# A graph network on one core: a sum moved one round later in VectorE's order, six result slots in the convolutions, a counting table of 128 by 784

## The chip, the core and the metric

The kernel runs on one core of a Trainium2 chip. A core has TensorE (matmuls and transposes into PSUM banks), VectorE, ScalarE, GpSimd (here it issues the indirect DMAs, gathers and scatters) and SyncE (it issues all other DMAs). Each engine works through its own instructions in order and waits on semaphores; 16 DMA engines move the data. The metric is the time of one launch in microseconds, the median of several runs.

## The reference

`x` has 100000 rows of 96 numbers; there are 50000 edges, sorted by destination. Four layers, each with a residual sum:

```python
edge_index = jnp.stack([src, dst])
h = jnp.maximum(_layernorm(x, axis=-1), 0.0)
x = x + _L0_gnn_ref(h, edge_index, edge_attr_32, ...)   # first edge layer
h = jnp.maximum(_layernorm(x, axis=-1), 0.0)
x = x + _L1_gnn_ref(h, ..., edge_attr_96, src, dst)     # second edge layer
h = jnp.maximum(_layernorm(x, axis=-1), 0.0)
x = x + _L2_gnn_ref(h, edge_index, W, b)                # convolution 0
h = jnp.maximum(_layernorm(x, axis=-1), 0.0)
x = x + _L3_gnn_ref(h, src, dst, ...)                   # convolutions 1, 2, 3
```

The first edge layer, where the moved sum lies (`h = x + update` there is the kernel's `y`):

```python
edge_input = jnp.concatenate([x[src], edge_attr], axis=-1)
messages = _gelu(edge_input @ mW1 + mb1) @ mW2 + mb2
gates = jax.nn.sigmoid(_gelu(edge_input @ gW1 + gb1) @ gW2 + gb2)
aggregated = jax.ops.segment_sum(messages * gates, dst, num_segments=x.shape[0])
combined = jnp.concatenate([x, aggregated], axis=-1)
update = _gelu(combined @ uW1 + ub1) @ uW2 + ub2
h = x + update
# then a layer norm of h with ln_g, ln_b
```

The convolutions gather a source row for each edge, scale it by the root of the source's degree, sum over the edges of a destination, apply a 96 by 96 weight and scale by the root of the destination's degree. Out-degrees and in-degrees are needed for all nodes.

## The kernel before, in words

**Stages, one after another.** Setup; counting (the degrees of all nodes as a table); the table's steps; a dense stage (all 100000 nodes as if they had no edges, in 196 groups); the two edge layers `e0`, `e1` and the four convolutions `conv[0]` to `conv[3]`, each over 98 groups of 512 edges (`G` = 4 columns of 128). Between stages a table in device memory (`t1`, `t2`, `c1`, `c2`) must be complete before the next stage gathers from it.

**The order.** `pipelined(eng, n, stages)` (L109) writes one engine's program as rounds: in round r it calls each stage function in the order of the list for group r - lag. So the lists are the order, and a function that waits holds everything behind it on that engine. `need(eng, count, value)` is a wait on a counter; `g.at(k)` is a slot of k; `landed`, `freed` give values of DMA counters.

**First edge layer, one round.** GpSimd gathers the source and destination rows, eight gathers of 128 rows a group (L598), at most five groups ahead of ScalarE's `norm`. VectorE: `times_g` (`yx`, L1214), `times_gate` (`msgT`, L1301), `new_x` (`xo`, L1336), `sums` (the scan into `aggT`, L1281), `edge_moments` (of the gathered rows), `new_y` (`y`, L1317, from PSUM bank 7), `with_b` (L1327), `moments_y`, then `of_round`: eleven short steps (L1148 to L1170) that give the roots `rstd`, `nmr` for the gathered rows and for `y` at once. ScalarE: `evac_d`, `update_act`, `hidden` (`g` L782, `m` L785), `edge_y` (`yg`, L722, needs the roots), `half_gate` (tanh, L796), `norms` (`hs`, `hd`, L687, need the roots), `evac_s`. TensorE: `hid`, `upd_u` (L993, the source of `new_y`), `messages`, `upd_z`, `tr`. SyncE stores `xo` at lag 10.

**Convolutions, one round.** GpSimd gathers four times (L598); ScalarE scales the rows (`rows_in`, L831 or L834); TensorE transposes them and after the scan (`sums`, L1281) applies the weight (L1017); VectorE's `finish` (L1415, L1422) writes the result into one of three slots of `xo`, for which it waits until the store of the group three before has landed (`x_out`, or in convolution 3 the four scatters, L673). SyncE loads `goes`, `idx` and, from convolution 1 on, `now` (`now_load`, L544: the degree roots of sources, plane 0, and destinations, plane 1, in one DMA for three groups, after `xr` of three groups ago) and stores at lag 9 (`conv_store`, L562). In convolutions 0 and 1 every third round has the eleven root steps (`row_roots`).

**Counting.** 392 rounds. A node number is split into `hi` and `lo` (shift and mask on integers, `LO` = 1024). VectorE compares `iota_lo` with `lo` (two comparisons of 1024 columns, L1081), ScalarE makes the row of `hi` (two squares L695, one relu L699, 128 columns wide), both into two buffers in turn; TensorE adds the products into four banks (four matmuls of 512 columns with 98 weight columns, L861). The table then takes some twenty steps on 98 partitions and 1024 columns (L1090 to L1125).

## Time and profile before

| | us |
|---|---|
| median of 3 runs | 7310.7 (7306.1 to 7322.6) |
| the profiled execution | 7306.9 |
| its span on the core | 7305.1 |
| busy: TensorE, VectorE, ScalarE, GpSimd | 4615.6, 4007.5, 3526.0, 4164.3 |
| first gather of the dense stage, of `e0`, of `e1` | 564.2, 2147.1, 3565.3 |
| first gather of conv 0, 1, 2, 3 | 4575.7, 5127.3, 5718.8, 6281.6 |

No engine is busy for more than 63% of the span, and the granted clock of TensorE is 0.716 on the mean. The stages have different limits, so shares over the whole span say little: each stage is read by itself, and in it what ends the idle time ahead of each engine's instructions.

### The profile page before, as it was taken

What the parts mean: (1) busy time and instruction counts of PE and PEld (TensorE: products, weight loads), DVE (VectorE), ACT (ScalarE), POOL (GpSimd) and SP (SyncE); (2) the same over time, 40 slices, a digit from 0 to 9 for tenths busy, and PEclk for the clock granted to TensorE, in tenths of its full rate; (3) what the DMA queues carried; (4) which work ended last, traced back from release to release, by engine and by line L of the source; (5) the groups of instructions that cost most, each with busy time, mean ns of one, the idle gap of its engine ahead of it and who ended that gap; (6) DMA issues with size and microseconds to landing.
All of it is one profiled execution on the core that took longest, in us unless ns stands there. A gap on an engine that the chain in (4) does not pass through costs nothing. (4 is left out here: it accounts for less than half of the span.)

```text
span 7305.1 us, 104580 instructions
## 1 busy us (share of the span) xinstructions
PE 4615.6 (63%) x19614; PEld 2994.2 (41%) x19614; DVE 4007.5 (55%) x12715; ACT 3526.0 (48%) x8822; POOL 4164.3 (57%) x4323
## 2 busy tenths in 40 slices
PE   6877888888876666666687888455445455322222
PEld 2335565556543333333344444344344344322222
DVE  5776777777765555555455555566555433322222
ACT  6886888888865555555455555222222122111110
POOL 0004555555447555554377776776666566677777
PEclk9997888998878877777688888555555555555555
DMA  0002333333332222222244444566444688533333
GB/s 15 0 0 77 100 102 103 101 105 100 100 89 69 62 60 58 61 61 59 64 118 118 120 120 110 142 159 157 102 115 112 102 122 121 93 72 78 76 80 72
DMA packets 956422, 652.69 MB, mean 89 GB/s; under 512 B 728867, under 2 KB 833199, under 8 KB 956232
## 3 DMA queue, kind: packets, MB, share of 16 engines
q1 hardware_dynamic: 818346, 483.05, 23.6%
q0 software_dynamic: 137984, 168.67, 14.6%
q8 instruction: 27, 0.44, 0.0%
q14 instruction: 65, 0.53, 0.0%
HBM read 420.24 MB, written 232.62 MB: 89 GB/s over the span
## 5 line engine op out<-in xcount | busy, mean ns | idle before, releaser
L1017 PE MATMUL bank<-w,aggT 96*128 96x96 f32 (+1 forms) x3136 | 790.2, 433 | 1343.8 <-DVE aggT L1281 1343.7
L598 POOL DMA_INDIRECT got<-info_d,idx x784 | 776.9, 991 | 1310.3 <-issue 779.5
L598 POOL DMA_INDIRECT xs<-t,idx x1176 | 1110.1, 944 | 626.7 <-issue 346.2
L1017 PEld LDWEIGHTS bank<-w,aggT 96*128 96x128 f32 (+1 forms) x3136 | 698.5, 328 | 1498.3 <-issue 1323.8
L598 POOL DMA_INDIRECT xs<-c,idx x784 | 756.9, 965 | 347.9 <-issue 233.3
L834 ACT ACTIVATE msg<-xs,now 128x96 f32<-128x96 f32 x784 | 227.7, 363 | 1340.0 <-DMA xs<-c,idx 535.3
L1281 DVE TENSOR_TENSOR_SCAN aggT<-goes,aggT,bank 96x512 f32<-96x512 f32 (+1 forms) x490 | 621.1, 1267 | 74.8 <-PE bank L977 45.4
L598 POOL DMA_INDIRECT xs<-in_x_dram,idx x392 | 375.5, 958 | 489.1 <-ACT hd L687 327.9
L687 ACT ACTIVATE hd<-xd,nmr,rstd 128x96 f32<-128x96 f32 x1568 | 599.2, 454 | 32.7 <-DVE nmr L1170 32.7
L1010 PE MATMUL bank<-ident,msg 128*96 128x128 f32 (+1 forms) x1568 | 420.3, 423 | 224.9 <-ACT msg L831 172.6
L935 PE MATMUL bank<-ident,hs 128*128 128x128 f32 (+1 forms) x784 | 173.5, 361 | 586.8 <-ACT hs L687 585.2
L1422 DVE SCALAR_TENSOR_TENSOR xo<-bank,now,rows 128x96 f32<-128x96 f32 x784 | 194.5, 311 | 551.1 <-DMA c<-xo 333.8
L1422 DVE SCALAR_TENSOR_TENSOR y<-bank,now,rows 128x96 f32<-128x96 f32 x392 | 97.3, 310 | 721.3 <-issue 370.9
L861 PE MATMUL bank<-xd,hot_hi 128*98 128x512 f16 x1568 | 407.3, 382 | 83.3 <-ACT hot_hi L699 69.9
L673 POOL DMA_INDIRECT out_dram<-xo,idx_out x392 | 390.2, 995 | 119.3 <-issue 119.3
L598 POOL DMA_INDIRECT xd<-in_x_dram,idx x392 | 381.8, 974 | 119.5 <-issue 119.2
L598 POOL DMA_INDIRECT xd<-t,idx x392 | 369.8, 943 | 119.5 <-issue 119.5
L1081 DVE TENSOR_SCALAR xd<-iota_lo,lo_of 128x1024 f16<-128x1024 f16 x784 | 345.9, 483 | 136.3 <-PE bank L861 129.5
L1010 PEld LDWEIGHTS bank<-ident,msg 128*96 128x96 f32 (+1 forms) x1568 | 317.2, 229 | 250.3 <-issue 138.7
L935 PEld LDWEIGHTS bank<-ident,hs 128*128 128x128 f32 (+1 forms) x784 | 107.5, 170 | 685.8 <-ACT hs L687 481.2
L687 ACT ACTIVATE hs<-xs,nmr,rstd 128x96 f32<-128x96 f32 x784 | 300.4, 455 | 152.2 <-DVE nmr L1170 151.6
L722 ACT ACTIVATE yg<-y,nmr,rstd 128x96 f32<-128x96 f32 x392 | 150.9, 455 | 447.2 <-DVE nmr L1170 447.2
(193 smaller groups left out, 10999.9 us busy)
## 6 DMA issues: line engine op xcount, KB each, us to landing
goes<-goes_d SPq DMA_DIRECT2D x392, 256.0 KB, 3.9
t<-xo SPq DMA_DIRECT2D x490, 192.0 KB
xd<-in_x_dram SPq DMA_DIRECT2D x196, 192.0 KB, 2.4
t<-xn SPq DMA_DIRECT2D x196, 192.0 KB
out_dram<-oo SPq DMA_DIRECT2D x196, 192.0 KB
goes<-goes_d SPq DMA_DIRECT2D x196, 192.0 KB, 3.4
xd<-t SPq DMA_DIRECT2D x196, 192.0 KB, 4.0
c<-xo SPq DMA_DIRECT2D x196, 192.0 KB
```

Of the source, the lines that this page charges most:

```text
L598: nc.gpsimd.indirect_dma_start(out=into, out_offset=None, in_=table, in_offset=bass.IndirectOffsetOnAxis(ap=indices, axis=0)).then_inc(don ...
L673: nc.gpsimd.indirect_dma_start(out=out[:, :], out_offset=bass.IndirectOffsetOnAxis(ap=idx_out[:, half(g), col + c:col + c + 1], axis=0), i ...
L687: ins = nc.scalar.activation(into[:, c, :], x[:, c, :], ACT.Relu, bias=nmr[:, b, q, c:c + 1], scale=rstd[:, b, q, c:c + 1])
L722: ins = nc.scalar.activation(yg[:, g.at(2), c, :], y[:, c, :], ACT.Identity, bias=nmr[:, b, q, c:c + 1], scale=rstd[:, b, q, c:c + 1])
L834: ins = nc.scalar.activation(msg[:, g.at(2), c, 0:D], xs[:, g.at(6), c, :], ACT.Relu, scale=scale[:, col + c:col + c + 1])
L861: ins = nc.tensor.matmul(bank[1 + 2 * which + side][0:HI, :], hot_hi[:, g.at(2), which, 0:HI], hot_lo[:, g.at(2), which, side * 512:side * ...
L935: ins = nc.tensor.transpose(bank[0][0:w, c * P:(c + 1) * P], hs[:, g.at(3), c, 0:w], ident[:])
L1010: ins = nc.tensor.transpose(bank[g.at(2)][0:m, c * P:(c + 1) * P], msg[:, g.at(2), c, 0:m], ident[:])
L1017: ins = nc.tensor.matmul(tok(bank[2 + g.at(2)], m)[:, c, :], aggT[0:m, g.at(3), c * P:(c + 1) * P], w2[:] if k == 0 else w3[:, k - 1, :], ...
L1081: nc.vector.tensor_scalar(hot_lo[:, g.at(2), which, :], iota_lo[:], lo_of[:, which, bass.ds(g.j, 1)], None, ALU.is_equal).then_inc(hot, 1)
L1281: nc.vector.tensor_tensor_scan(aggT[0:m, s, :], goes[0:m, s, :], source(g), aggT[0:m, before, GE - 1:GE], ALU.mult, ALU.add)\
L1422: ins = nc.vector.scalar_tensor_tensor(out=to, in0=u[:, c, 0:D], scalar=now[:, half(g), 1, col + c:col + c + 1], in1=rows[:, 1 + k, :], op ...
```

## The change

**First edge layer.** On VectorE `new_y` and `moments_y` work on group r - 4 instead of r - 3 and stand first and third in the round; `edge_moments` stands between them; `times_g` and `new_x` work on r - 5 instead of r - 4. ScalarE's `edge_y` goes to lag 4, SyncE's store of `xo` to lag 11, the root steps run for one more round at the end.

**Convolutions.** Results go into the six slots of `xn` instead of the three of `xo` (counters `c_out`, in convolution 3 `scattered` with six slots). `now_load` becomes two DMAs: `ns_load` (plane 0, lag 1, behind ScalarE's `h` of three groups ago) and `nd_load` (plane 1, lag 5, behind `xr` of three groups ago).

**Counting.** `HI, LO` = 128, 784; the matmuls have 392 columns (`SIDE`) and 128 weight columns, VectorE's comparisons 784, the table's steps 784 on 128 partitions. `hi` and `lo` come from a multiplication, a rounding by adding and subtracting 1.5 x 2^23 and a multiply-add, instead of integer shifts and masks.

The core of the diff:

```diff
-HI, LO = 98, 1024
+HI, LO = 128, 784
+SIDE = LO // 2
...
-            slots = dict(gathered)
+            slots = dict(gathered, c_out=(6, 1, 1))
...
-                def now_load(g):
+                def ns_load(g):
+                    if g.c % GT == 0:
+                        n = G * (GT if g.turn is not None else min(GT, EG - g.j))
+                        need(sp, ph["h"], g.j - 3)
+                        sp.sem_inc(sp_turn, 1)
+                        sp.dma_start(now[:, half(g), 0, 0:n], norms_of[:, 0, bass.ds(g.j * G, n)])\
+                            .then_inc(ph["ns_in"][half(g)].sem, 16)
+
+                def nd_load(g):
...
                         need(sp, ph["xr"], g.j - 3)
                         sp.sem_inc(sp_turn, 1)
-                        sp.dma_start(now[:, half(g), :, 0:n], norms_of[:, :, bass.ds(g.j * G, n)])\
-                            .then_inc(ph["now_in"][half(g)].sem, 16)
+                        sp.dma_start(now[:, half(g), 1, 0:n], norms_of[:, 1, bass.ds(g.j * G, n)])\
+                            .then_inc(ph["nd_in"][half(g)].sem, 16)
...
-                stages += [(now_load, 3)] if k > 0 else []
-                stages += [(conv_load, 4)]
+                stages += [(ns_load, 1)] if k > 0 else []
+                stages += [(conv_load, 4)] + ([(nd_load, 5)] if k > 0 else [])
...
-                    standard(ph, g, y[:, g.at(2), :, :], 3, 2)
+                    standard(ph, g, y[:, g.at(2), :, :], 4, 2)
...
                         ins = nc.tensor.matmul(
-                            bank[1 + 2 * which + side][0:HI, :], hot_hi[:, g.at(2), which, 0:HI],
-                            hot_lo[:, g.at(2), which, side * 512:side * 512 + 512],
+                            bank[1 + 2 * which + side][0:HI, 0:SIDE], hot_hi[:, g.at(2), which, 0:HI],
+                            hot_lo[:, g.at(2), which, side * SIDE:side * SIDE + SIDE],
...
-            for which, st in enumerate((st_s, st_d)):
-                nc.vector.tensor_single_scalar(lo_i[:, which, :], st[:], LO - 1, ALU.bitwise_and)
-                nc.vector.tensor_single_scalar(hi_i[:, which, :], st[:], LO.bit_length() - 1, ALU.arith_shift_right)
+            nc.vector.tensor_scalar(hi_of[:], cols[:, 0:2, :], 1.0 / LO, -BELOW, ALU.mult, ALU.add)
...
-            nc.vector.tensor_copy(lo_of[:], lo_i[:])
-            nc.vector.tensor_copy(hi_of[:], hi_i[:])
+            nc.vector.tensor_scalar(lo_of[:], hi_of[:], NEAREST, None, ALU.add)
...
+            nc.vector.tensor_scalar(hi_of[:], lo_of[:], -NEAREST, None, ALU.add)
...
-                    stages = [(times_g(ph), 4), (times_gate, 2), (new_x, 4), (sums, 2), (edge_moments, 0), (new_y, 3),
-                              (with_b, 0), (moments_y, 3), (of_round, 0, EG + 3)]
+                    stages = [(new_y, 4), (edge_moments, 0), (moments_y, 4), (times_g(ph), 5), (times_gate, 2), (new_x, 5),
+                              (sums, 2), (with_b, 0), (of_round, 0, EG + 4)]
...
-                    col, o = g.c % GT * G, g.at(3)
+                    col, o = g.c % GT * G, g.at(6)
...
-                        need(dve, ph["x_out"][o], freed(g, 3))
+                        need(dve, ph["c_out"][o], freed(g, 6))
                     dve.sem_inc(dve_turn, 1)
                     if k > 0:
-                        need(dve, ph["now_in"][half(g)], landed(g, 6))
+                        need(dve, ph["nd_in"][half(g)], landed(g, 6))
```

## Rows read from the trace of the kernel before

**Rows 1.** Busy us (xinstructions) by stretch: counting, e0, e1, conv 1, 2, 3; clock.

```profile
200.00:400.00 200.00, 168.73 (x654) 67.36 (x652) 143.41 (x326) 177.42 (x489) 0.00 (x0) 1.00 0.00 0
2300.00:3300.00 1000.00, 663.15 (x1984) 330.26 (x1982) 525.32 (x1628) 558.92 (x1270) 554.53 (x581) 0.78 0.26 62
3700.00:4400.00 700.00, 569.53 (x2509) 331.76 (x2509) 370.45 (x1265) 375.35 (x840) 529.16 (x561) 0.86 0.48 119
5200.00:5600.00 400.00, 203.18 (x828) 167.11 (x826) 235.29 (x782) 100.66 (x275) 262.23 (x278) 0.50 0.46 115
5780.00:6200.00 420.00, 215.89 (x903) 182.17 (x901) 164.83 (x380) 87.07 (x303) 291.00 (x309) 0.50 0.90 120
6400.00:7200.00 800.00, 221.20 (x927) 187.04 (x927) 210.93 (x462) 90.08 (x308) 612.33 (x617) 0.50 0.37 78
```

**Rows 2.** Groups of instructions, ScalarE, 2300 to 3300: busy, mean ns, idle before.

```profile
L722 ACT ACTIVATE yg<-y,nmr,rstd 128x96 f32<-128x96 f32 x284 | 109.3, 455 | 322.1 <-DVE nmr L1170 322.1
```

**Rows 3.** Timeline of GpSimd: start, us, instruction, idle before; e1's and conv 0's first gathers.

```profile
3565.31 0.94 POOL L598 DMA_INDIRECT xs<-t,idx  x1 [108.38 <-DMA idx<-at]
3566.56 0.94 POOL L598 DMA_INDIRECT xs<-t,idx  x1 [0.30 <-issue]
...
4575.65 0.94 POOL L598 DMA_INDIRECT xs<-t,idx  x1 [31.98 <-DMA idx<-at]
```

**Rows 4.** Timeline of one round of the first edge layer, in part.

```profile
2709.64 1.03 PE L993 MATMUL bank<-uw,u 97*128 97x96 f32 x8
...
2710.85 0.55 DVE L1317 TENSOR_TENSOR y<-hd,bank 128x384 f32<-128x384 f32 x1 [3.97 <-PE bank L993]
...
2714.97 1.18 ACT L722 ACTIVATE yg<-y,nmr,rstd 128x96 f32<-128x96 f32 x3 [4.45 <-DVE nmr L1170]
```

**Rows 5.** Instructions of L598: ns min/median/max, first and last start; e0's source rows.

```profile
L598 POOL DMA_INDIRECT xs<-in_x_dram,idx x392: 938/944/1936, 2147.1 to 3451.0; - x196
```

**Rows 6.** Timeline of counting, in part: at the low clock, then at the full one.

```profile
54.05 0.20 PEld L861 LDWEIGHTS bank<-xd,hot_hi 128*98 128x98 f16 x1 [0.22 <-issue]
54.48 0.20 PEld L861 LDWEIGHTS bank<-xd,hot_hi 128*98 128x98 f16 x1 [0.22 <-issue]
...
301.54 0.69 ACT L695 ACTIVATE apart<-iota_hi,hi_of 128x128 f32<-128x128 f16 x2 [0.21 <-PE bank L861]
302.64 0.69 ACT L695 ACTIVATE apart<-iota_hi,hi_of 128x128 f32<-128x128 f16 x2
304.00 0.40 ACT L695 ACTIVATE apart<-iota_hi,hi_of 128x128 f32<-128x128 f16 x1 [0.21 <-PE bank L861]
...
530.00 1.04 PE L861 MATMUL bank<-xd,hot_hi 128*98 128x512 f16 x4
```

**Rows 7.** Timeline of the table's steps: the first and the last of 1024 columns.

```profile
539.48 2.29 DVE L1094 TENSOR_TENSOR_SCAN xn<-xo,xn 98x1024 f32<-98x1024 f32 x1
...
557.33 1.23 DVE L1125 SCALAR_TENSOR_TENSOR hdT<-xs,xd 98x1024 f32<-98x1024 f32 x1
```

**Rows 8.** Timeline of VectorE in convolution 1: `finish` of three rounds.

```profile
5401.28 0.99 DVE L1422 SCALAR_TENSOR_TENSOR xo<-bank,now,rows 128x96 f32<-128x96 f32 x4 [4.07 <-DMA c<-xo]
...
5407.12 0.99 DVE L1422 SCALAR_TENSOR_TENSOR xo<-bank,now,rows 128x96 f32<-128x96 f32 x4 [0.69 <-issue]
...
5412.01 0.99 DVE L1422 SCALAR_TENSOR_TENSOR xo<-bank,now,rows 128x96 f32<-128x96 f32 x4 [2.18 <-PE bank L1017]
```

**Rows 9.** Waits in convolution 2, 5780 to 6200: us in total, times, longest.

```profile
ACT msg L834 <- DMA now<-norms_of: 173.4, 25, 9.9
DVE xo L1422 <- DMA c<-xo: 165.6, 34, 7.8
```

**Rows 10.** Timeline of VectorE in convolution 2: `finish` of two rounds.

```profile
5901.56 0.99 DVE L1422 SCALAR_TENSOR_TENSOR xo<-bank,now,rows 128x96 f32<-128x96 f32 x4 [2.18 <-PE bank L1017]
...
5905.92 0.99 DVE L1422 SCALAR_TENSOR_TENSOR xo<-bank,now,rows 128x96 f32<-128x96 f32 x4 [2.18 <-PE bank L1017]
```

**Rows 11.** DMA queues in convolution 2, 5780 to 6200: packets, MB, share of 16 engines.

```profile
q0 software_dynamic: 9877, 15.20, 58.5%
```

More of the change, by code:

```diff
@@ L314, in build @@
         for k in range(4):
-            slots = dict(gathered)
+            slots = dict(gathered, c_out=(6, 1, 1))
+            slots.pop("x_out")
             if k in (0, 3):
@@ L318, in build @@
             if k > 0:
-                slots["now_in"] = (2, 1, GT)
+                slots["ns_in"] = (2, 1, GT)
+                slots["nd_in"] = (2, 1, GT)
             if k == 3:
-                slots.pop("x_out")
+                slots.pop("c_out")
                 slots["out_in"] = (2, 1, GT)
-                slots["scattered"] = (3, G, 1)
+                slots["scattered"] = (6, G, 1)
             counts = dict(h=1, seg=1, agg=1, u=1, xr=1)
@@ L521, in _ @@
                     source = e1 if k == 0 else conv[0]
-                    for s in range(3):
-                        need(sp, source["x_out"][s], ended(EG, 3, s))
+                    out_of, many = ("x_out", 3) if k == 0 else ("c_out", 6)
+                    for s in range(many):
+                        need(sp, source[out_of][s], ended(EG, many, s))
                 def conv_load(g):
@@ L551, in out_load @@
                             was = g.shift(i)
-                            if g.turn is not None or g.c >= 2 * GT:
-                                need(sp, ph["scattered"][was.at(3)], freed(was, 3, G) - 16 * G)
+                            need(sp, ph["scattered"][was.at(6)], freed(was, 6, G))
                             sp.sem_inc(sp_turn, 1)
@@ L574, in _ @@
                         need(sp, ph["xs"][s], ended(EG, 6, s, G))
+            for s in range(6):
+                need(sp, conv[1]["c_out"][s], ended(EG, 6, s))
+                need(sp, conv[2]["c_out"][s], ended(EG, 6, s))
+                need(sp, conv[3]["scattered"][s], ended(EG, 6, s, G))
             for s in range(3):
-                need(sp, conv[1]["x_out"][s], ended(EG, 3, s))
-                need(sp, conv[2]["x_out"][s], ended(EG, 3, s))
-                need(sp, conv[3]["scattered"][s], ended(EG, 3, s, G))
                 need(sp, dn["o_out"][s], ended(NG, 3, s))
@@ L644, in _ @@
                 before_ph = e1 if k == 0 else conv[k - 1]
+                out_of, many = ("x_out", 3) if k == 0 else ("c_out", 6)
+                for s in range(many):
+                    need(pool, before_ph[out_of][s], ended(EG, many, s))
                 for s in range(3):
@@ L647, in _ @@
                         need(pool, dn["x2_out"][s], ended(NG, 3, s))
-                    need(pool, before_ph["x_out"][s], ended(EG, 3, s))
                     if k == 3:
@@ L826, in rows_in @@
                         need(act, ph["xs"][g.at(6)], landed(g, 6, G))
-                        need(act, ph["now_in"][half(g)], landed(g, 6))
+                        need(act, ph["ns_in"][half(g)], landed(g, 6))
                         scale = now[:, half(g), 0, :]
@@ L1370, in _ @@
                 before_ph = e1 if k == 0 else conv[k - 1]
-                for s in range(3):
-                    need(dve, before_ph["x_out"][s], ended(EG, 3, s))
+                out_of, many = ("x_out", 3) if k == 0 else ("c_out", 6)
+                for s in range(many):
+                    need(dve, before_ph[out_of][s], ended(EG, many, s))
                 nc.vector.memset(aggT[:, 2, GE - 1:GE], 0.0).then_inc(idx_step, 1)
```

49 lines of the change are left out of this document (25 added, 24 removed).

## The prediction

> **What bounds the kernel now.** I read the stages first (busy time of each engine in a stretch of each stage), because the chain that ended last covers only the last stage. Counts give the rates: GpSimd issues 8 gathers for a group in an edge layer, 4 in convolutions 0 to 2, 8 gathers and scatters in convolution 3. In the first edge layer ScalarE writes `yg` 284 times in 1000 us [rows 2], 4 to a group, so 71 groups and 14.08 us each. In the second, 561 issues in 700 us are 70.1 groups, 9.98 us each [rows 1]. Convolution 1 takes 400/(278/4) = 5.76 us, convolution 2 420/(309/4) = 5.44 us, convolution 3 800/(617/8) = 10.37 us [rows 1]. A gather occupies GpSimd 0.94 us and the next starts 0.30 us later (1.25 us from start to start) [rows 3], so 8 cost 9.98 us and 4 cost 4.99 us: the second edge layer and convolution 3 run at GpSimd's issue rate and can't be quickened by what the other engines do; the first edge layer lies 4.1 us over it, convolution 1 0.77 us, convolution 2 0.45 us. The counting stage has no GpSimd work at all.
>
> Then I read what closes each loop. In the first edge layer (one round) TensorE's `u` of L993 starts at 2709.64; VectorE, idle for 3.97 us, starts `y` (L1317) at 2710.85, then moments and the eleven short steps of the roots, and only at 2714.97, after 4.45 us of idleness, may ScalarE write `yg` [rows 4]. Over 71 rounds that idleness is 322.1 us, 4.54 us a round [rows 2]. VectorE stands waiting for TensorE in the middle of its round while ScalarE waits for VectorE: a serial loop, no full engine.
>
> **First edge layer.** `new_y`, `moments_y` move to the front and one group back: they take `u` of the group that TensorE finished in its round before. The roots no longer wait for this round's `u`. Nothing is added: the same instructions, one more drain round. What is late next is ScalarE itself: of 1000 us it is busy 558.9 and waits 322.1 for roots [rows 1, 2], the other 119 us are waits for TensorE in its own round. Without the wait for roots a round is (558.9 + 119)/71 = 9.55 us. VectorE: `new_y` now heads its in-order queue, with the moments of the gathered rows, `yx`, the gate product, `xo` and the scan behind it. Before it waits, `u` has long been due: L993 started at 2709.64 and took 1.03 us, so it ends at 2710.67 [rows 4], about where ScalarE ends `m` and would start the next `yg`. From there VectorE has 525/71 = 7.4 us of work [rows 1] and about a microsecond of steps between; some 8.4 us, under 9.55. TensorE is busy 663/71 = 9.3 us at a granted clock of 0.78 [rows 1], 7.3 us if all of it ran at full clock, so it fits into 9.98 us as long as its clock is above 0.73; in the second edge layer it was 0.86 [rows 1]. So the bound is GpSimd, 9.98 us. It now runs up to five groups ahead, which absorbs rounds that are longer than the mean. The stage runs from the first gather at 2147.1 [rows 5] to the second layer's first at 3565.31, 1418 us [rows 3]. The second layer, at that same rate, takes 4575.65 - 3565.31 = 1010 us, of which 98 x 9.98 = 978 are issue and 32 are drain [rows 3]. The first layer's drain has more and longer rounds; I take 52 us. 978 + 52 = 1030, so **-388 us**. Ends: -400 (drain as short as the second layer's, less the added round) and, since each 0.5 us of round is 49 us, -300 if ScalarE's round comes to 10.9.
>
> **Counting stage.** Two buffers are passed around between ScalarE and VectorE, which fill them, and TensorE. ScalarE's squares start at 301.54, 302.64 and 304.00: 1.10 us where it is free, 2.46 us for two rounds [rows 6]. Of these 2.46 TensorE's four matmuls are 1.04 [rows 6] and ScalarE's squares and relu 1.1; 0.3 us are handing over, and the last start waited 0.21 us for TensorE [rows 6]. At the low clock a matmul of 512 columns follows the last after 0.43 us [rows 6], so after 0.215 at the full one; 392 columns are 0.77 of that, 0.165, so four of them save 0.20 us, and the pair of rounds becomes 2.26 us. ScalarE's own floor is 2 x 1.10 = 2.20, so nothing more is to be had from VectorE's shorter comparison (1024 to 784 columns), which ends before the relu anyway. 0.10 us x 392 rounds = **-39 us**. Ends: -50 (ScalarE's floor) and 0, should the weight loads (98 columns, now 128; 0.20 us each with 0.22 us of idleness between two at the low clock [rows 6]) come out from behind the shorter matmuls. The clock was 1.00 all through with TensorE busy 169 of 200 us [rows 1]; it will be less busy, which is a rival below.
>
> The Trainium skill (TensorE: Matmul & The Clock Gate, Back-to-back issue gap) states about 131 ns a matmul for a sustained stream with N = 512 and 81 with N = 128, so some 115 for 392 (an estimate between them): four would save 0.06 us instead of 0.20, the stage 13 us instead of 39. This trace's 0.215 us speaks against it. Its section LDWEIGHTS has a load grow with its columns, 82 to 107 ns; exposed in full that would take back 0.1 us of the 0.2; no run here shows it yet.
>
> **Table and columns.** The 1024-wide steps run from 539.48 to 558.56, 19.1 us [rows 7]; 784 columns on 128 partitions are 0.77 of that: -4.5, with the evictions **-5 us**. The column steps exchange eight short instructions for four wider ones before counting: no more than 1 us either way, taken as zero.
>
> **Convolutions.** Convolution 1: VectorE waited 4.07 us for the store `c<-xo` (slot of three rounds ago) where its neighbours waited 2.18 us for TensorE [rows 8]. Starts of `finish`: 5407.12 to 5412.01 is a round without either, 4.89 us; 5401.28 to 5407.12 one with roots, 5.84 us [rows 8]. Two and one make 5.21 us a group: (5.76 - 5.21) x 98 = **-54 us**; ends -75 (GpSimd's 4.99) and -20, should most of the store's wait come back as one for `u`. Six slots take the store out, since it then has three more rounds; `ns_load` no longer stands behind the results' `xr` on SyncE's queue, `nd_load` does, but three groups ahead of its reader. Splitting one DMA in two adds one issue (0.65 us for the double one) per three groups to SyncE, beside 15 us of round: nothing. Convolution 2: store waits 165.6 us and scale waits 173.4 us in 420 us [rows 9], VectorE's bare round 4.36 us [rows 10], so GpSimd's 4.99 us would bind; but the 16 DMA engines are busy 0.90 of the time, 58.5% with the gathers [rows 1, 11], and at 4.99 us would be 0.98. I take 5.1: **-33 us**; ends -43 and 0. Convolution 0 waits for TensorE, not for stores, and convolution 3 is at GpSimd's rate: zero each. Dense stage and second edge layer: untouched.
>
> **Sum.** 388 + 39 + 5 + 54 + 33 = 519 us off the profiled execution's 7306.9 gives 6788; the median of the runs is 4 us higher: **6790 us**.
>
> **Rivals.**
> - ScalarE binds the first edge layer. Its margin is 0.43 us, and `tanh`, now right behind `yg`, may wait for TensorE's gate product when the clock is low. At 10.9 us a round: +90, 6880 us. For it: 0.78 of clock; against: four idle microseconds of TensorE vanish from the round. 0.17.
> - The wait stays in part: VectorE, whose gate product and scan stand behind `yg` and in front of the roots, gives them out 2 us late. 11.7 us: +170, 6960 us. 0.08.
> - The convolutions give nothing, because the store's wait turns into another of the same length: +87, 6877 us. 0.08.
> - The edit does not bite (the wait for `u` comes back one group later): counting, table and convolutions only, 7180 us. 0.03.
> - **Slower**: the granted clock. In convolution 1, TensorE busy half the time, it stood at 0.50 [rows 1]. If the lighter counting rounds and the first edge layer ran at 0.50, matmuls there would be 0.43 us apart at 512 columns (starts of weight loads 54.05 and 54.48) [rows 6], 0.33 at 392; two rounds 2.9 us, +88 us for the stage; TensorE's 7.3 us would be 14.6 in the edge layer, +50. With the convolutions' 87 and the table off: 7355 us. It decides once TensorE's clock in the edge layer is under 0.52 and counting's at 0.50. 0.03.
> - The forecast: 0.60. The last 0.01 is left over.
>
> **Numbers.** The forecast's best ends give 6735; the rivals at 6877 and 6880 must lie inside, with some margin: 6720 to 6920. A measurement of this kernel can tell about 0.2%: faster 0.95, the same 0.01, slower 0.04.
>
> **What would show it.** First edge layer: ScalarE's wait for `nmr` before `yg` nearly gone, group 10.0 us, GpSimd as busy as in the second. Counting: two rounds 2.25 us at clock 1.00. Convolutions 1 and 2: no `c<-` wait at VectorE. Wrong if `yg` still waits 2 us or more, or if `hs` or `tanh` waits for TensorE instead, or if the clock in the first layer is below 0.73.

## The result, and the profile after

The changed kernel takes **6882.8 us** (median of 4 runs, 6878.0 to 6904.2) where the kernel before took 7312.7 beside it: ratio 0.942 (95% interval 0.940 to 0.945). The forecast was 6790, its range 6720 to 6920: the sign and the range hold, but 93 us of the gain are missing. The profiled execution of the changed kernel has a span of 6876.1 us.

Busy time by stretch, as in [rows 1] (us and instruction counts of TensorE, weight loads, VectorE, ScalarE, GpSimd; clock, DMA share, GB/s). The stages come earlier now, so the stretches are shifted: counting, first edge layer (800 us), second edge layer, convolutions 1, 2, 3.

```profile
200.00:400.00 200.00, 146.53 (x712) 56.95 (x713) 134.97 (x357) 194.11 (x536) 0.00 (x0) 1.00 0.00 0
2300.00:3100.00 800.00, 622.61 (x2002) 303.98 (x2001) 524.46 (x1637) 562.33 (x1287) 626.16 (x571) 0.86 0.34 76
3400.00:4100.00 700.00, 552.86 (x2498) 325.37 (x2499) 370.91 (x1267) 375.76 (x839) 529.17 (x561) 0.88 0.48 119
4850.00:5250.00 400.00, 229.99 (x936) 189.20 (x936) 264.97 (x885) 114.58 (x313) 298.29 (x316) 0.50 0.54 130
5400.00:5820.00 420.00, 235.34 (x952) 192.35 (x950) 174.33 (x395) 92.45 (x316) 301.81 (x320) 0.50 0.99 126
6000.00:6800.00 800.00, 213.84 (x936) 192.74 (x936) 211.88 (x466) 91.25 (x312) 610.22 (x623) 0.50 0.37 79
```

Counting: 536 instructions of ScalarE in 200 us, three to a round, so 1.119 us a round where [rows 1] give 489 and 1.227; the clock stayed at 1.00. First edge layer: 571 gathers in 800 us are 71.4 groups, 11.2 us each. The forecast was 9.98, and the second layer has it as before: 561 in 700. The first edge layer's 571 gathers keep GpSimd busy for 626 us, **1.10 us each**, where the second layer has 529.17/561 = 0.943. With the 0.30 us between two, 626 + 571 x 0.30 = 797 of 800 us: GpSimd is full. It is the bound that was forecast, but it is slower than its rate elsewhere. Convolution 1: 400/(316/4) = 5.06 us a group (before 5.76), convolution 2: 420/(320/4) = 5.25 (before 5.44), convolution 3: 800/(623/8) = 10.27 (before 10.37).

The wait that the moved sum was to remove, as in [rows 2], but in 800 us:

```profile
L736 ACT ACTIVATE yg<-y,nmr,rstd 128x96 f32<-128x96 f32 x288 | 110.9, 455 | 143.4 <-DVE nmr L1182 142.9 <-DVE rstd L1179 0.5
```

It fell from 4.54 us a round to 143.4/72 = 1.99. It is no longer part of the loop that sets the pace: VectorE itself waits for gathers, as the next rows show (waits from 2200 to 3100: us in total, times, longest).

```profile
DVE mv L1207 <- DMA xd<-in_x_dram,idx: 271.5, 80, 4.1
ACT yg L736 <- DVE nmr L1182: 160.9, 79, 3.8
```

The first gather of the second edge layer, as in [rows 3]; then counting at full clock and the table's first and last wide step, as in [rows 6, 7]; then `finish` in convolution 1, as in [rows 8]:

```profile
3235.94 0.94 POOL L610 DMA_INDIRECT xs<-t,idx  x1 [43.62 <-DMA idx<-at]
```

```profile
301.10 0.69 ACT L709 ACTIVATE apart<-iota_hi,hi_of 128x128 f32<-128x128 f16 x2
301.29 0.82 PE L875 MATMUL bank<-xd,hot_hi 128*128 128x392 f16 x4 [0.32 <-ACT hot_hi L713]
303.34 0.69 ACT L709 ACTIVATE apart<-iota_hi,hi_of 128x128 f32<-128x128 f16 x2
...
496.71 1.79 DVE L1106 TENSOR_TENSOR_SCAN xn<-xo,xn 128x784 f32<-128x784 f32 x1
...
511.09 0.98 DVE L1137 SCALAR_TENSOR_TENSOR hdT<-xs,xd 128x784 f32<-128x784 f32 x1
```

```profile
5105.71 0.99 DVE L1435 SCALAR_TENSOR_TENSOR xn<-bank,now,rows 128x96 f32<-128x96 f32 x4 [2.19 <-PE bank L1031]
...
5111.51 0.99 DVE L1435 SCALAR_TENSOR_TENSOR xn<-bank,now,rows 128x96 f32<-128x96 f32 x4 [0.66 <-issue]
5116.40 0.99 DVE L1435 SCALAR_TENSOR_TENSOR xn<-bank,now,rows 128x96 f32<-128x96 f32 x4 [2.18 <-PE bank L1031]
```

Two counting rounds are 2.24 us (before 2.46), four matmuls 0.82 (1.04). The table takes 15.4 us (19.1). In convolution 1 a round with roots is 5.80 us here and one without 4.89, as before; the round that stood for the store, a third of them at 6.5 to 7.3 us before, is gone.

Stage by stage, from the first gather of one stage to that of the next (the first row is the first gather itself):

| us | before | after | difference | forecast |
|---|---|---|---|---|
| counting, table (to the first gather) | 564.2 | 516.8 | -47 | -44 |
| dense | 1582.9 | 1576.9 | -6 | 0 |
| first edge layer | 1418.2 | 1142.3 | **-276** | **-388** |
| second edge layer | 1010.3 | 1010.5 | 0 | 0 |
| convolution 0 | 551.6 | 550.8 | -1 | 0 |
| convolution 1 | 591.5 | 530.3 | -61 | -54 |
| convolution 2 | 562.8 | 533.2 | -30 | -33 |
| convolution 3 | 1023.5 | 1015.4 | -8 | 0 |
| sum | | | -429 | -519 |

One term carries the miss: the first edge layer, 112 us. The 6 us of the dense stage aren't a gain of the change: over the runs outside experiments 9 to 12, all with this same dense stage, it takes 1564 to 1583 us.

### The profile page after: what moved, and what is told of

It reads as the page before. It is cut to its first block and busy times, and to the rows that moved or that the text cites. A ratio compares the mean times of both kernels' runs of the same rounds, so it can differ in the third digit from the quotient of the medians.

```text
span 6876.1 us, 104878 instructions
## 1 busy us (share of the span) xinstructions
PE 4438.8 (65%) x19614; PEld 2908.5 (42%) x19614; DVE 3951.5 (57%) x12722; ACT 3522.4 (51%) x8822; POOL 4259.0 (62%) x4323
## 5 line engine op out<-in xcount | busy, mean ns | idle before, releaser
L1031 PE MATMUL bank<-w,aggT 96*128 96x96 f32 (+1 forms) x3136 | 773.9, 428 | 470.5 <-DVE aggT L1293 470.4
L1024 PEld LDWEIGHTS bank<-ident,msg 128*96 128x96 f32 (+1 forms) x1568 | 290.1, 218 | 1052.0 <-ACT msg L848 678.8
L610 POOL DMA_INDIRECT xs<-in_x_dram,idx x392 | 473.3, 1207 | 173.9 <-issue 119.2
L1207 DVE BATCH_NORM_STATS2 mv<-xs 128x6 f32<-128x192 f32 x392 | 122.9, 355 | 752.4 <-DMA xd<-in_x_dram,idx 353.9
L687 POOL DMA_INDIRECT out_dram<-xn,idx_out x392 | 390.4, 996 | 119.4 <-issue 119.1
L1435 DVE SCALAR_TENSOR_TENSOR xn<-bank,now,rows 128x96 f32<-128x96 f32 x784 | 194.5, 311 | 395.1 <-PE bank L1031 358.6
L875 PE MATMUL bank<-xd,hot_hi 128*128 128x392 f16 x1568 | 324.8, 329 | 124.0 <-ACT hot_hi L713 115.7
L949 PE MATMUL bank<-ident,hs 128*128 128x128 f32 (+1 forms) x784 | 151.4, 325 | 376.3 <-ACT hs L701 374.8
L1093 DVE TENSOR_SCALAR xd<-iota_lo,lo_of 128x784 f16<-128x784 f16 x784 | 297.0, 421 | 143.6 <-PE bank L875 143.5
L888 PE MATMUL bank<-hdT,uw 96*96 96x512 f32 x392 | 249.1, 721 | 179.2 <-ACT hdT L746 179.2
```

The source lines that it names most:

```text
L610: nc.gpsimd.indirect_dma_start(out=into, out_offset=None, in_=table, in_offset=bass.IndirectOffsetOnAxis(ap=indices, axis=0)).then_inc(don ...
L687: nc.gpsimd.indirect_dma_start(out=out[:, :], out_offset=bass.IndirectOffsetOnAxis(ap=idx_out[:, half(g), col + c:col + c + 1], axis=0), i ...
L875: ins = nc.tensor.matmul(bank[1 + 2 * which + side][0:HI, 0:SIDE], hot_hi[:, g.at(2), which, 0:HI], hot_lo[:, g.at(2), which, side * SIDE: ...
L888: nc.tensor.matmul(into, w, x, start=True, stop=True).then_inc(done.sem, 1)
L949: ins = nc.tensor.transpose(bank[0][0:w, c * P:(c + 1) * P], hs[:, g.at(3), c, 0:w], ident[:])
L1024: ins = nc.tensor.transpose(bank[g.at(2)][0:m, c * P:(c + 1) * P], msg[:, g.at(2), c, 0:m], ident[:])
```

## Where it went: gathers whose issue is held

A gather's issue takes 0.944 or 0.945 us at the median in every stage but convolution 3 (0.950). In the first edge layer of the changed kernel single ones take up to 2.88. I call a gather held if its issue takes over 1.0 us. Instructions by line: ns min/median/max, first and last start.

```profile
L610 POOL DMA_INDIRECT xd<-in_x_dram,idx x391: 940/945/1378, 2100.2 to 3191.4; - x196
L610 POOL DMA_INDIRECT xs<-in_x_dram,idx x388: 940/945/2881, 2103.9 to 3184.5; - x194
```

The second edge layer of the same kernel:

```profile
L610 POOL DMA_INDIRECT xd<-t,idx x388: 940/944/955, 3250.9 to 4213.8; - x194
L610 POOL DMA_INDIRECT xs<-t,idx x385: 940/945/958, 3249.7 to 4208.8; - x193
```

Counted over the first edge layer, 142 of 784 gathers take over 1.0 us, 119.9 us more than 0.944 each; 119.9/98 = 1.22 us a group, and 9.98 + 1.22 = 11.2. That is the whole excess. In the kernel before it was 57 gathers and 17.5 us, and cost nothing, since GpSimd waited for ScalarE's `norm` there: 327.9 us, in the second row. The dense stage has held gathers as well, 167 of 784 with 36.6 us in all and 1.34 us at most (164 and 37.1 us before); they cost nothing either, since GpSimd waits there. The gathers of source rows in the first edge layer, after and before: count, busy and mean ns, idle time before.

```profile
L610 POOL DMA_INDIRECT xs<-in_x_dram,idx x392 | 473.3, 1207 | 173.9 <-issue 119.2
```

```profile
L598 POOL DMA_INDIRECT xs<-in_x_dram,idx x392 | 375.5, 958 | 489.1 <-ACT hd L687 327.9
```

And what lies beside a held one (timeline of the changed kernel, GpSimd and VectorE):

```profile
2699.10 0.94 POOL L610 DMA_INDIRECT xs<-in_x_dram,idx  x1 [0.30 <-issue]
...
2699.62 0.54 DVE L1226 TENSOR_TENSOR yx<-yg,rows 128x384 f32<-128x384 f32 x1
...
2700.35 2.81 POOL L610 DMA_INDIRECT xs<-in_x_dram,idx  x1 [0.30 <-issue]
...
2700.67 0.54 DVE L1348 TENSOR_TENSOR xo<-yx,xn 128x384 f32<-128x384 f32 x1
...
2701.14 1.27 DVE L1293 TENSOR_TENSOR_SCAN aggT<-goes,aggT,msgT 96x512 f32<-96x512 f32 x1
...
2702.34 0.52 DVE L1339 TENSOR_TENSOR xn<-xd,rows 128x384 f32<-128x384 f32 x1
...
2702.79 0.37 DVE L1160 TENSOR_SCALAR var<-mv 128x12 f32<-128x12 f32 x1
...
2703.47 0.94 POOL L610 DMA_INDIRECT xd<-in_x_dram,idx  x1 [0.30 <-issue]
```

VectorE runs `xo`, the scan and `xn` without a pause, each with both sources in SBUF; the gather that began 0.32 us before them ends 0.3 us after them, at 2703.16, and the short `var` behind them takes 0.37 us where the steps like it take 0.17. In the second edge layer the large instructions of VectorE have one source in PSUM. So the **theory**: while VectorE reads two operands from SBUF, GpSimd's issue of a gather stands (the expectations call it the port theory). The **rivals**: VectorE's load as such, whatever its operands; DMA traffic (the queue theory); ScalarE's round (the first rival of the prediction, which would give the same 6880 us).

Not every gather beside such an instruction is held. Of the 784 gathers, 549 have none of the four (`yx`, `xo`, the scan, `xn`) beside their first 0.944 us, and one of these is held (beside L1283, a single instruction with two SBUF sources too). Of the other 235, 141 are held. It depends on how far the gather has come: `xo` starts 0.12 to 0.38 us into a gather 92 times, and all 92 are held; `yx` starts 0.31 to 0.57 us into one 92 times, and none is. The gather at 2699.10 above is such a one, its 0.94 us unchanged although `yx` starts 0.52 us into it. So of the four instructions three hold a gather in this kernel.

The Trainium skill (SBUF — State Buffer, section "Who interferes with whom") says that a VectorE instruction with two inputs in SBUF contends with a GpSimd instruction that reads SBUF, for a pair of ports that is an exclusive lock. With that rule the trace agrees: a gather reads its row numbers (`idx`) from SBUF, and all 142 held ones lie beside an instruction with two SBUF sources. The same section reports a probe in which `tensor_tensor` didn't stall DMA, and infers as the reason that making descriptors needs only the pair's write side. Here gathers are held beside `tensor_tensor` and the scan, up to 2.88 us, and for them the measurement decides; whether it is the read of `idx` or the making of the descriptors that stands, no run here separates.

## Experiments

All ratios are to the kernel before, run beside them. It took 7336 us beside experiments 1 to 4 and 7318 beside 5 to 8, where the times in the expectations reckon from 7311 to 7313: the ratios and the stages are what to compare. The first four take the change apart, the next four test the theory, the last four were to settle what was left.

**1. The moved sum alone** on the kernel before:

```diff
-                    stages = [(times_g(ph), 4), (times_gate, 2), (new_x, 4), (sums, 2), (edge_moments, 0), (new_y, 3),
-                              (with_b, 0), (moments_y, 3), (of_round, 0, EG + 3)]
+                    stages = [(new_y, 4), (edge_moments, 0), (moments_y, 4), (times_g(ph), 5), (times_gate, 2), (new_x, 5),
+                              (sums, 2), (with_b, 0), (of_round, 0, EG + 4)]
```

> The kernel before with the first edge layer's part of the change alone. If the 276 us by which that stage shrank in the changed kernel (1142 us from its first gather to the next layer's, 1418 before) are all its own, this kernel takes 276 us less than before, about 7035 us, and a group in that stage takes 11.2 us, with the fourth source gather of a group over 1.5 us long. The theory of the prediction (a plain issue rate of 9.98 us a group, minus 388 us) would want about 6925 us.

Measured: 7053.0 us, ratio 0.962 (0.959 to 0.964), 283 us off; first edge layer 1134 us, 11.18 us a group, a gather's mean there 1086 ns. The other stages are as before within 3 us, but for convolution 2: 583 us here, 578 in experiment 3, 563 in the profile of the kernel before, all three with the same code in it. The gain and the missing part are both of this edit: neither the slots nor the table touches them.

**2. The convolutions' part alone,** six slots and the load of the degree roots in two:

```diff
-            slots = dict(gathered)
+            slots = dict(gathered, c_out=(6, 1, 1))
+            slots.pop("x_out")
```

> The kernel before with the convolutions' part alone (six slots, two loads of norms). In the changed kernel convolution 1 was 61 us shorter, convolution 2 30 us, convolution 3 8 us: minus 99, about 7214 us. If the gain in the convolutions needed the rest of the change, it is smaller; the prediction had minus 87.

Measured: 7228.0 us, 0.985 (0.984 to 0.987), 109 us off. Convolution 1 is 531 us (593 and 594 in experiments 1 and 3, which have three slots and ran beside it), convolution 2 555 (583 and 578), convolution 3 1016 (1024 and 1023). Convolution 3's 8 us thus belong to this part: there 72 gathers over 1.0 us in the kernel before (10.5 us in all) are 7 in the changed kernel, while the scatters are as before (188 and 185 over 1.0 us). What held these gathers wasn't looked into.

**3. The counting table alone:**

```diff
-HI, LO = 98, 1024
+HI, LO = 128, 784
```

> The kernel before with the counting table alone (128 by 784). The first gather of the dense stage came 47 us earlier in the changed kernel: about 7265 us, two counting rounds in 2.24 us, the granted clock 1.00 in 200 to 400 us. The rival of a fallen clock would have two rounds at 2.9 us and 7390 us.

Measured: 7284.2 us, 0.993 (0.991 to 0.994), 52 us off; first gather at 517.8 (before 564.2). The three parts make 283 + 109 + 52 = 444 us, the whole change 430: within the noise they add up.

**4. The whole change without the split load:** six slots, but `now` loaded by one DMA as before.

```diff
-                stages += [(ns_load, 1)] if k > 0 else []
-                stages += [(conv_load, 4)] + ([(nd_load, 5)] if k > 0 else [])
+                stages += [(now_load, 3)] if k > 0 else []
+                stages += [(conv_load, 4)]
```

> The changed kernel with the one load of both norms as before (one DMA at lag 3 behind the results of three groups ago) and six result slots. If convolution 1 gains by its slots alone, it still takes 530 us from its first gather to the next one's; convolution 2, where ScalarE waited for the norms (173 us in 420 us before), gives back some of its 30 us. By the theory that the slots do it all: 6883 us. By the theory that the early load of the norms carries convolution 2: 6900 to 6915 us.

Measured: 6900.5 us, 0.940 (0.938 to 0.942), against 0.942 for the whole change. Convolution 1 is 531 us and convolution 2 554, as in experiment 2 (531 and 555), which has the split load and ran beside it. Six slots do all of it; the split load gives nothing that can be measured. The 6900 us lie at the edge of what was expected if the load carried convolution 2, but the kernel before was 24 us slower beside it too.

**5 and 6. Three more instructions of VectorE in each round of the second edge layer**, where no gather was held. Kernel 5 gives them two sources in SBUF; kernel 6 is the same but for one source in PSUM. They compute nothing that is used.

```diff
+                    def extra(g):
+                        for i, to in enumerate((yg[:, 0, :, :], yg[:, 1, :, :], yx[:])):
+                            nc.vector.tensor_tensor(to, y[:, 0, :, :], y[:, 1, :, :], ALU.mult)  # 6: tok(bank[3])
```

> The changed kernel with three more VectorE instructions at the end of each round of the second edge layer, back to back, 128 x 384, both sources in SBUF, results unused. VectorE has room for them there (365 of 700 us busy). Port theory (a gather's issue on GpSimd is held while VectorE works through instructions with two SBUF sources): they hold one gather in many of the rounds, a group goes from 9.99 to 10.4 us or more, plus 40 us or more for the stage. Queue theory (the gathers of the first layer are held because descriptors or DMA engines back up at its pace): no gather is held, the stage stays at 1011 us, 6883 us in all.

> The same three instructions with one of the two sources in PSUM (a bank that this layer doesn't use). Port theory: no gather is held, a group takes 9.99 us as in the changed kernel, 6883 us. Rival (any busy VectorE holds GpSimd, or the added work lengthens the loop): as slow as with both sources in SBUF.

Measured: 6936.5 us (0.948, 0.947 to 0.950) and 6898.5 (0.943, 0.941 to 0.944). The second edge layer is 1059.7 and 1010.3 us. Two views of kernel 5, then the same two of kernel 6: the stretch 3300 to 4100, columns as above, and the layer's gathers of destination rows (ns min/median/max, first and last start).

```profile
3300.00:4100.00 800.00, 645.24 (x2737) 370.81 (x2736) 509.57 (x1603) 408.75 (x913) 614.28 (x610) 0.82 0.46 113
```

```profile
L610 POOL DMA_INDIRECT xd<-t,idx x384: 940/945/1516, 3251.3 to 4253.7; - x192
```

```profile
3300.00:4100.00 800.00, 661.05 (x2895) 383.25 (x2895) 535.34 (x1686) 432.20 (x967) 604.78 (x641) 0.85 0.48 119
```

```profile
L610 POOL DMA_INDIRECT xd<-t,idx x389: 940/944/953, 3250.0 to 4218.7; - x195
```

With the sources in SBUF 156 gathers are held and the group takes 10.52 us; with one of them in PSUM none is held and it takes 9.99, though VectorE does *more* work in the 800 us (535 against 510) and DMA moves more (119 against 113 GB/s). One operand decides; VectorE's load and DMA traffic are out as causes, and both expectations of the port theory were met.

**7. Another order** in the first edge layer, so that the instructions with two sources in SBUF don't stand in one row:

```diff
-                    stages = [(new_y, 4), (edge_moments, 0), (moments_y, 4), (times_g(ph), 5), (times_gate, 2), (new_x, 5),
-                              (sums, 2), (with_b, 0), (of_round, 0, EG + 4)]
+                    stages = [(new_y, 4), (edge_moments, 0), (with_b, 0), (moments_y, 4), (times_g(ph), 5), (new_x, 5),
+                              (times_gate, 2), (sums, 2), (of_round, 0, EG + 4)]
```

> The changed kernel with another order in VectorE's round of the first edge layer: the sum with b ahead of y's moments, xo ahead of the gate product, so that between instructions with two SBUF sources stands one with a source in PSUM or the moments; the longest run falls from 2.3 us (xo, scan, b) to 1.3 us (scan alone). Port theory: a held gather waits 1.3 us at most instead of 1.9, a group falls from 11.2 to 10.3 to 10.8 us, 6790 to 6840 us. Queue theory: 11.2 us, 6883 us. If ScalarE's loop bound it instead: no change either.

Measured: 6893.7 us, 0.943 (0.941 to 0.944), no gain; 11.17 us a group. My expectation for the port theory, 10.3 to 10.8, was wrong; by its pace alone the run fits the queue theory, which experiments 5 and 6 exclude.

```profile
L610 POOL DMA_INDIRECT xd<-in_x_dram,idx x386: 940/944/1801, 2099.4 to 3171.6; - x193
L610 POOL DMA_INDIRECT xs<-in_x_dram,idx x384: 940/947/1685, 2101.9 to 3166.3; - x192
```

The longest hold is shorter (1.80 us, not 2.88), but 261 gathers are held instead of 142, 112 us instead of 120. Which instructions hold has changed: `yx`, beside which no gather was held, now lies beside 76 held ones. That the sum came out nearly the same isn't explained: the four instructions run 2.9 us a round in both kernels and hold GpSimd for 1.2 of them, and no run shows that this share is fixed.

**8. The scan's message source in PSUM:** the gated product is written back over the bank that it reads.

```diff
-                    nc.vector.scalar_tensor_tensor(out=msgT[:, g.at(2), :], in0=tanh_g[:, g.at(2), :], scalar=1.0,
+                    nc.vector.scalar_tensor_tensor(out=bank[4][0:D, :], in0=tanh_g[:, g.at(2), :], scalar=1.0,
...
-                    sums = sums_of(ph, lambda g: msgT[:, g.at(2), :], ph["msg"], D, ph["z"])
+                    sums = sums_of(ph, lambda g: bank[4][0:D, :], ph["msg"], D, ph["z"])
```

> The changed kernel with the gated messages written over TensorE's product in its PSUM bank instead of into SBUF, so that the scan (1.27 us) has one SBUF source; TensorE's next product there waits for the scan. Port theory: what is left of the run is b's sum (0.5 us) alone and yx and xo, a group 10.0 to 10.4 us, 6765 to 6805 us. Queue theory: 11.2 us. Rival (the longer hold of the bank closes a new loop): over 11.2 us.

Measured: **6849.5 us**, 0.937 (0.935 to 0.940); first edge layer 1093.6 us, 10.74 us a group, the fastest version found (kernels 6 and 7, run beside it, have 0.943). The gain is there, but my 10.0 to 10.4 us and 6765 to 6805 us were too low.

```profile
L610 POOL DMA_INDIRECT xs<-in_x_dram,idx x392 | 431.4, 1100 | 172.7 <-issue 119.2
```

A gather's mean fell from 1207 to 1100 ns, the time held from 119.9 to 69.9 us. The stage gave back 49 us by one instruction of 1.27 us a round; `yx`, `xo` and `xn` still have both sources in SBUF. The theory isn't complete, though: 57 gathers still take over 1.5 us, 2.12 at most. The one that starts at 2660.23 takes 2.07 us, beside `xo` (from 2660.52, 0.55 us) and the scan (from 2660.99, 1.27 us), and ends with the scan, which now reads one source from PSUM and holds no gather in the second edge layer. Why a hold that began with `xo` can last through it wasn't settled.

**9 and 10. All large instructions of the first edge layer without a second SBUF source.** Kernel 9 is kernel 8 with `times_g`, `new_x`, `with_b` in one row; kernel 10 reads one source of each from PSUM.

```diff
-... tensor_tensor(yx[:], yg[:, g.at(2), :, :], wide(rows[:, 0, :]), ALU.mult)
-... tensor_tensor(xn[:, g.at(6), :, :], xd[:, g.at(6), :, :], wide(rows[:, 1, :]), ALU.add)
-... tensor_tensor(xo[:, g.at(3), :, :], yx[:], xn[:, g.at(6), :, :], ALU.add)
+... tensor_tensor(yx[:], yg[:, g.at(2), :, :], tok(bank[4]), ALU.mult)
+... tensor_tensor(xn[:, g.at(6), :, :], xd[:, g.at(6), :, :], tok(bank[4]), ALU.add)
+... tensor_tensor(xo[:, g.at(3), :, :], yx[:], tok(bank[4]), ALU.add)
```

> The changed kernel with the sum's message source of the first edge layer in PSUM, as in after_psum, and VectorE's round there put in another order: new_y, edge_moments, moments_y, times_gate, times_g, new_x, with_b, sums. The three instructions with two sources in SBUF (times_g, new_x, with_b) now follow one another. It is the kernel that e0_row_psum is to be compared with. The port theory: their total is what it was, so the first edge layer stays at 10.7 to 11.0 us per group (after_psum 10.74), its stage at 1090 to 1115 us, the kernel at 6845 to 6875 us, and single gathers are held longer (over 2.2 us, the whole length of the three) while fewer are held. If instead only the scan held GpSimd, the group would be 10.74 and gathers would be held beside the scan alone.

> e0_row_sbuf with one operand changed in each of the three VectorE instructions of the first edge layer that have two sources in SBUF: times_g reads the token products in PSUM in place of the weight row, with_b reads them in place of the bias row, new_x in place of xn. Shapes, types and counts are the same; the new x of that layer is thus computed from other numbers, and the message product waits for the with_b of the round before it. Port theory (GpSimd's issue of a gather is held while VectorE reads two operands from SBUF): no or hardly any gather held beyond 1.0 us, mean of a gather's issue 0.944 to 0.96 us, 9.98 to 10.1 us per group, the stage at 1018 to 1035 us and the kernel some 60 to 80 us under e0_row_sbuf, near 6780 us. Rival 1 (VectorE's load or GpSimd's waits for norm set the 10.7, whatever the operands): the period stays within 0.1 us of e0_row_sbuf. Rival 2 (the ring's DMA traffic holds the issue): the same number of gathers held as in e0_row_sbuf. Rival 3: ScalarE's loop of about 10.0 us and the added wait take the place: gathers not held, period over 10.3 us, with GpSimd idle before its gathers.

These two, and 11 and 12, ran on another chip than the runs above, and there the kernel *before* takes 9314 us instead of 7313. Instructions of VectorE, ScalarE and GpSimd last as long as elsewhere, but in the dense stage of kernel 12 VectorE stands 63 times for a release that the profile doesn't show ("remote"), 705.9 us in all, some 11 us about every 35 us, and TensorE with it, for up to 10 us; the granted clock is 0.64 there (700 to 1900 us), where the changed kernel had 0.89. Timeline of the dense stage in kernel 12, which is the changed kernel up to convolution 1:

```profile
1023.14 0.64 PE L917 MATMUL bank<-ident,hs 128*96 128x128 f32 x4 [0.36 <-ACT hs L702]
1033.06 0.63 DVE L1208 BATCH_NORM_STATS2 mv<-bank 128x6 f32<-128x192 f32 x2 [12.21 <-remote]
1033.10 0.59 ACT L747 ACTIVATE hdT<-bank 96x512 f32<-96x512 f32 x1 [8.74 <-remote]
1033.74 2.02 PE L889 MATMUL bank<-hdT,uw 96*96 96x512 f32 x2 [9.96 <-ACT hdT L747]
```

So their times (9350.3 us, ratio 1.004, 1.003 to 1.006; and 9359.9, 1.005, 1.003 to 1.007) say little about our question: of the expected 60 to 80 us between them nothing appeared, and GpSimd stands waiting for hundreds of microseconds in both. In the stage itself kernel 10 is even slower, 1616 against 1577 us; how much of that is the wait that it adds isn't separated. What can be read are the gathers themselves, by the view of one line's instructions: the layer's source and destination rows in kernel 9, then in kernel 10.

```profile
L610 POOL DMA_INDIRECT xs<-in_x_dram,idx x392: 938/944/1339, 2791.7 to 4292.1; - x196
L610 POOL DMA_INDIRECT xd<-in_x_dram,idx x392: 940/944/1585, 2797.0 to 4297.4; - x196
```

```profile
L610 POOL DMA_INDIRECT xs<-in_x_dram,idx x392: 938/944/1214, 2776.1 to 4312.0; - x196
L610 POOL DMA_INDIRECT xd<-in_x_dram,idx x392: 940/944/953, 2781.4 to 4317.0; - x196
```

Held: 47 gathers in kernel 9, **one** of 784 in kernel 10 (1.21 us, beside the L1286 that adds `found` and `in_tab`, both in SBUF). The quarter of fastest groups takes 9.99 us or less in kernel 10 and 10.3 or less in kernel 9. The theory's mechanism holds in the first edge layer too; its price for the whole kernel rests on experiments 5, 6 and 8. My expectation for kernel 9 (fewer gathers held, each over 2.2 us) was wrong in size: none is over 1.6.

**11. Experiments 7 and 8 together**, a candidate for a faster version:

> after_psum with VectorE's order in the first edge layer as in after_order: with_b ahead of moments_y, and new_x ahead of times_gate, so that the instructions with two sources in SBUF stand apart. It is the candidate for the fastest version. If the sum of the two-source time counts (as after_order showed, which gained nothing), the stage is that of after_psum, 1094 us within 10, and the kernel 6840 to 6865 us. If with the scan's source in PSUM the shorter stretches fit into GpSimd's slack between gathers, the group falls to 10.3 to 10.5 us, the stage to 1050 to 1070 us, the kernel to 6805 to 6825 us.

Measured, on the chip with the stops: 9367.4 us, 1.006 (1.004 to 1.007); first edge layer 1585 us against 1577 in kernel 9, 51 gathers held. Neither expectation is decided.

**12. Another address in convolutions 2 and 3:** edges whose source has no in-edges read spread rows instead of one common row.

```diff
-            nc.vector.tensor_scalar(at[:, 5, :], found[:, 0, :, 0], float(E_PAD), None, ALU.min)
+            nc.vector.tensor_scalar(is_last[:], found[:, 0, :, 0], 0.5, -0.5 * E_PAD, ALU.mult, ALU.add)
+            nc.vector.tensor_tensor(is_last[:], is_last[:], in_tab[:], ALU.add)
+            nc.vector.tensor_tensor(at[:, 5, :], found[:, 0, :, 0], is_last[:], ALU.min)
```

> The changed kernel with one address changed: in the third and fourth convolution a gathered edge whose source has no in-edges reads a row of the table that depends on the edge, where in the kernel as changed all of these read the same one row. The outputs of these convolutions differ thereby. Theory (packets that read the one row at the same time take long, so the queue's time and not the instruction count sets the third convolution): GpSimd's gather packets there fall from 786 ns to 215 to 350 ns, the DMA share from 0.86 to 0.4 to 0.6, the third convolution from 5.23 to 5.0 to 5.1 us per group (stage 533 to 555 now, 515 to 525 then), and its length no longer differs from run to run. Rival: the packets are slow because of the load that other transfers make, or slow and without a consequence; the stage stays at 530 to 555 us.

Measured: 9225.6 us, 0.991 (0.988 to 0.993). Convolution 2, 7500 to 8000, first two views of kernel 9 (common row), then the same two of kernel 12: busy times as above, and the gathers' queue with packets, MB and its share of the 16 DMA engines.

```profile
7500.00:8000.00 500.00, 201.18 (x840) 169.83 (x840) 151.33 (x346) 82.97 (x284) 278.33 (x296) 0.50 0.58 94
```

```profile
q0 software_dynamic: 9479, 14.58, 33.2%
```

```profile
7500.00:8000.00 500.00, 211.62 (x886) 178.79 (x884) 160.93 (x370) 86.51 (x296) 275.47 (x292) 0.50 0.39 97
```

```profile
q0 software_dynamic: 9312, 14.32, 14.1%
```

The common row does make packets slow on the mean: as many packets take less than half the DMA time when the rows are spread. But the stage is 700 us against 681 to 689 in kernels 9 to 11: no gain, so the rival in its second form (slow and without a consequence) holds, on this chip. On the others, where the DMA share of convolution 2 is 0.98 to 1.02 with six slots, it wasn't tried.

This kernel is also the only view of the changed first edge layer on that chip: 1457 us, while in kernels 9 to 11, whose message product waits for the scan, it is 1577 to 1616. Kernels 9 and 11, which are kernel 8 in other orders, are thus slower than the kernel before on this chip (1.004 and 1.006), where the changed kernel, with experiment 12's address, keeps 0.991. Kernel 8 itself wasn't run there, and neither was a profile of the kernel before taken, so where the rest of the change's gain goes on this chip stays open.

## Why the prediction was right or wrong

- **What bounds the first edge layer, and that the moved sum bites: right.** A serial loop through TensorE and VectorE was broken, and GpSimd's issue took over. TensorE's clock went from 0.78 to 0.86, ScalarE's wait for the roots went from 4.54 to 2.0 us a round.
- **First edge layer, -388: the term was mis-sized, -276.** The step that failed is "so the bound is GpSimd, 9.98 us": the engine is right, its rate isn't. It was taken from the second edge layer, as if an engine's issue rate were a constant. It isn't: in the first layer VectorE has four large instructions with two SBUF sources in each round; three of them hold gathers, 1.22 us a group, 120 us in all, and the group takes 11.2 us. [Rows 5] had the hint: a maximum of 1936 ns for a gather beside a median of 944, in a layer where GpSimd was idle enough to hide it. The drain was 44 us (43.62 in the row above) against the 52 I took, which gave 8 back.
- **Its lower end of -300** was for ScalarE at 10.9 us a round; the stage came out beyond it, and the kernel's time inside 6720 to 6920 only because the range was drawn to hold the rivals at 6877 and 6880. The first rival's 6880 us fits the measured time to 3 us and is still not what happened: at 11.2 us a round ScalarE is busy for 7.9 and waits 2.0 for roots, VectorE waits for gathers, and moving one operand to PSUM quickened the layer with ScalarE's work unchanged.
- **The prediction's own mark**, "wrong if `yg` still waits 2 us or more", was reached (1.99 us a round in one stretch, 160.9/79 = 2.04 in the longer one), and its own sign of a "group 10.0 us" didn't come. As a sign the wait had lost its meaning: it is slack of a round that another engine stretches.
- **Counting, -39: right**, 0.108 us a round, 42 us. A matmul of 392 columns follows the last after the 0.165 us that the columns gave, within the rows' reading, with 128 weight columns no dearer: a load is 0.096 us long on the mean in the trace, where it was 0.123 with 98. The Trainium skill's spacing for a sustained stream (TensorE: Matmul & The Clock Gate, Back-to-back issue gap), 131 ns at 512 columns and 81 at 128, and with it a gain of 13 us instead of 42, didn't show: at the full clock the matmuls start 0.215 us apart before and 0.165 after. The dearer load by its section LDWEIGHTS didn't show either. **Table, -5: -4.**
- **Convolution 1, -54: right**, -61; the group came to about 5.1 us, not 5.21, since the rounds with roots alternate between about 5.4 and 5.8 us, where I took 5.84 for all of them. **Convolution 2, -33: right**, -30 here, and 23 to 29 where both were run beside each other (554 and 555 us with six slots, 578 and 583 with three). The DMA share went to 0.99 as reckoned, but already at 5.25 us a group, not 5.1. From 5.44 that is 19 us; the rest of the 30 came at the stage's ends, so the fit of the number is partly luck.
- **Convolution 3, zero: off by 8 us**, in a term that I called GpSimd's rate. Again the rate wasn't constant: 987 ns a gather before, 965 after, which over 392 gathers is the 8 us.
- The rivals "edit doesn't bite", "convolutions give nothing" and "slower by the clock" didn't occur: counting stayed at 1.00, the first edge layer rose to 0.86.

## What to carry to other kernels

When one engine is forecast to become the bound, don't take its rate from a stage where its neighbours do other things. Look at the maximum of its instruction times in the very stage: held instructions hide while the engine has slack, and they cost once it has none. For a GpSimd that issues gathers, count VectorE's instructions with two sources in SBUF, and see whether one source can be left in PSUM; the one other order that was tried gained nothing.

## What the runs showed of the hardware

- A gather's issue on GpSimd, 0.944 us alone, stretched to 2.88 us beside three VectorE instructions with two SBUF sources. With one source of each in PSUM it stayed at 0.95 (second edge layer: 10.52 against 9.99 us a group; first: 47 held gathers against one).
- Whether a gather is held depended on when the instruction starts: at 0.12 to 0.38 us into the gather 92 of 92 were held, at 0.31 to 0.57 us none of 92.
- Gathers that read one common row cost more than twice the DMA time of as many that read spread rows (33.2% against 14.1% of the 16 engines), without a consequence for the stage where it was tried.
- One chip ran the kernel before 27% slower (9314 against 7313 us), by stops of some 11 us of VectorE about every 35 us of the dense stage, in which engines wait for something that the profile doesn't name. Instruction times of VectorE, ScalarE and GpSimd are unchanged, and the granted clock of TensorE is lower (0.64 against 0.89 in that stage). Its cause is open.
